# Shared-expert pieces of the last two images of a scan, mixture-of-experts and attention kernel, placed at other steps of the order

## The reference

```
x = x + scan(layernorm(x))          # 16 states per channel, h = exp(dt*a)*h + dt*b*x over 512 tokens
x = x + moe(layernorm(x))           # 64 experts, top 6, capacity 64 tokens per expert
x = x + attention(layernorm(x))     # 16 query heads, 4 key heads, causal
x = x + moe(layernorm(x))           # the same weights as the first time
...
def moe(hidden):
    y = routed experts: silu(x @ w_gate[e]) * (x @ w_up[e]) @ w_down[e], weighted and summed
    shared = silu(hidden @ sw_gate) * (hidden @ sw_up) @ sw_down      # inner width 704
    return y + shared
```

## Time and profile before

| | before |
|---|---|
| median of three runs | 3010.05 us |
| profiled execution | 3011.85 us, span 3010.0 us |
| TensorE busy | 2721.4 us (90%) |
| VectorE busy | 1790.6 us (59%) |
| GpSimd busy | 1529.4 us (51%) |
| ScalarE busy | 1298.4 us (43%) |
| last of the scans starts | 1044.7 us |
| experts' first transposes (L1116) start | 1116.60 us |
| end of the first experts on TensorE | about 1512 us |
| DMA, mean over the span | 188 GB/s |

### The profile page before, as it was taken

The page is one execution under the profiler, slowest core; times in us unless marked ns, Lnnn a source line. Parts: engine busy times, 40 slices in busy tenths (PEclk is TensorE's granted clock), DMA queues, the critical chain, the costliest instruction groups (busy, mean ns, idle before and its releaser), DMA issues.

```text
span 3010.0 us, 37439 instructions
## 1 busy us (share of the span) xinstructions
PE 2721.4 (90%) x13484; PEld 1435.5 (48%) x13484; DVE 1790.6 (59%) x3787; ACT 1298.4 (43%) x2689; POOL 1529.4 (51%) x944
## 2 busy tenths in 40 slices
PE   4658888998998879999969999999899999999998
PEld 2445554555555534433335555555544444444443
DVE  5899999999999852222246666665524444222222
ACT  4557585775857411111127767666712220111111
POOL 6999999999999901222135555554400001121211
PEclk7669999998999889999989999999999999999999
DMA  5454645545455379999930000001135324899997
GB/s 191 149 169 139 202 168 169 187 147 197 163 183 165 131 273 367 396 393 393 387 112 1 29 29 29 29 29 56 49 100 194 118 75 163 307 377 341 361 338 217
DMA packets 168234, 566.13 MB, mean 188 GB/s; under 512 B 22832, under 2 KB 24752, under 8 KB 167536
## 3 DMA queue, kind: packets, MB, share of 16 engines
q1 hardware_dynamic: 149904, 521.65, 46.9%
q0 software_dynamic: 17088, 40.90, 5.9%
q10 hardware_dynamic: 1056, 1.18, 0.1%
HBM read 487.89 MB, written 75.79 MB: 187 GB/s over the span
## 4 chain that ended last, share of the span: by engine, by line
PE 54%; ACT 3%; DVE 2%; POOL 2%; DMA 1%; issue 1%; POOLq 0%; SPq 0%; DVEq 0%; ACTq 0%
PE bank L1133 10%; PE bank L1159 5%; PE bank L1071 5%; PE bank L1036 5%; PE bank L1057 5%; PE bank L1184 5%; PE bank L1241 4%; PE bank L1218 3%; PE bank L1206 2%; PE bank L1230 2%; POOL arena L1940 2%; PE bank L1116 1%; PE bank L1172 1%; ACT arena L1763 1%; PE bank L1043 1%
## 5 line engine op out<-in xcount | busy, mean ns | idle before, releaser
L1844 POOL TENSOR_TENSOR arena<-arena 128x1024 f32<-128x1024 f32 x256 | 607.0, 2372 | 6.1 <-PE bank L986 3.0
L1692 ACT ACTIVATE bank<-arena 128x512 f32<-128x512 f32 x512 | 346.7, 689 | 317.9 <-DVE arena L1330 198.5
L986 PE MATMUL bank<-arena 128*128 128x128 f32 x2048 | 303.9, 301 | 147.3 <-POOL arena L1850 147.2
L1940 POOL TENSOR_TENSOR arena<-arena 128x2048 f32<-128x2048 f32 (+3 forms) x128 | 296.9, 2323 | 274.7 <-DVE arena L1560 274.6
L986 PEld LDWEIGHTS bank<-arena 128*128 128x128 f32 x2048 | 258.2, 155 | 233.5 <-POOL arena L1850 188.2
L1763 ACT ACTIVATE arena<-arena 128x256 f32<-128x256 f32 (+3 forms) x512 | 287.2, 566 | 148.3 <-DVE arena L1551 125.8
L1850 POOL TENSOR_TENSOR arena<-arena 128x512 f32<-128x512 f32 x256 | 333.6, 1304 | 17.5 <-DVE arena L1330 17.5
L1133 PE MATMUL bank<-arena 128*64 128x352 f32 x2048 | 327.2, 474 | 0.0
L1330 DVE TENSOR_TENSOR_SCAN arena<-bank,arena 128x512 f32<-128x512 f32 x256 | 310.7, 1214 | 25.9 <-POOL arena L1844 18.9
L1330 DVE TENSOR_TENSOR_SCAN bank<-bank,arena 128x512 f32<-128x512 f32 x256 | 308.4, 1205 | 0.0
L1057 PE MATMUL bank<-arena 128*128 128x512 f32 x640 | 288.3, 593 | 7.6 <-ACT arena L1719 7.6
(11 more groups left out here) (145 smaller groups left out, 4156.5 us busy)
## 6 DMA issues: line engine op xcount, KB each, us to landing
arena<-scratch_bc SPq DMA_DIRECT2D x128, 1024.0 KB, 5.4
arena<-in_w_out SPq DMA_DIRECT2D x128, 768.0 KB, 16.3
arena<-in_w_gate SPq DMA_DIRECT2D x128, 704.0 KB
arena<-in_w_up SPq DMA_DIRECT2D x128, 704.0 KB
scratch_x<-arena SPq DMA_DIRECT2D x16, 1024.0 KB, 4.5
scratch_xn<-arena SPq DMA_DIRECT2D x15, 1024.0 KB, 4.1
arena<-scratch_x SPq DMA_DIRECT2D x44, 256.0 KB, 6.1
arena<-scratch_x SPq DMA_DIRECT2D x8, 1024.0 KB, 7.5
```

What stands on the lines that cost most here:

```text
L986: i = nc.tensor.matmul(y[:, t * P:(t + 1) * P], w[:, n, t * P:(t + 1) * P], p.ident, is_transpose=True, start=False, stop=g == GROUPS - 1 ...
L1692: nc.scalar.activation(bank[p.da_bank(k, n)][:, :], block_of(p.dt, b, c), ACT.Exp, scale=p.alog[:, c, state:state + 1]).then_inc(*p.decaye ...
L1844: nc.gpsimd.tensor_tensor(out=p.hb[k % HB], in0=over(block_of(p.dtx, b, c), 1, NG), in1=p.bc[k // 2 % NBC][:, 0], op=ALU.mult).then_inc(*p ...
L1940: nc.gpsimd.tensor_tensor(out=own, in0=own, in1=over(p.rden[:, k % 2, :], 2, width), op=ALU.mult).then_inc(*p.divided.up(k))
```

## The change

The steps at which shared pieces stand become a table by image, `SHARED_AT`. Images 0 to 4 keep theirs. For image 5 the fourth down piece stands at step 46 instead of 51. For image 6 (the seventh) all gate and up pieces stand at steps 12 to 26 of the last batch, one at a time, and its down pieces at 29, 30, 33 and 34; the last two fall behind the last scan step, into the chain. In the chain, twelve pieces are made instead of eight: `sd` 2 and 3 of image 6, then `sg` and `su` of j = 0 to 4 of image 7. Five units are left for the experts' stage: j = 5, and t = 0 to 3 of image 7. The places at which products are read in the chain move with them. In the changed file every line behind the table is five to six lines further down.

```diff
+SHARED_AT = [(GATES, UPS, DOWNS)] * (BATCH - 3)
+SHARED_AT += [(GATES, UPS, (40, 41, 43, 46)), ((12, 15, 17, 20, 23, 26), (13, 16, 18, 21, 24, 26), (29, 30, 33, 34))]
...
-MADE_BESIDE = {"stats": 2, "logit": 1, "pick0": 1, "pick4": 1, "merge": 1, "lists": 1}
-TAKEN_BESIDE = {"rstd": ("silu",), "apply": ("hid",), "route_exp": ("silu",), "masks": ("hid",), "pick4": ("so",),
-                "merge": ("so",), "lists": ("so",)}
+MADE_BESIDE = {"stats": 2, "logit": 2, "pick0": 2, "pick4": 1, "merge": 2, "lists": 3}
+TAKEN_BESIDE = {"logit": ("so",), "route_max": ("so",), "route1": ("silu",), "pick1": ("silu", "hid"),
+                "merge": ("silu", "hid"), "lists": ("silu", "hid")}
...
+    gates, ups, downs = SHARED_AT[q]
     for j in range(SC):
-        yield GATES[j], ("sg", 0, q, j)
...
+        yield gates[j], ("sg", 0, q, j)
...
     products = [i for i in left if i[0] in ("sg", "su", "sd")]
+    products += [(kind, 0, BATCH - 1, j) for j in range(SC) for kind in ("sg", "su")]
+    products = products[:sum(MADE_BESIDE.values())]
```

More of the change, by code:

```diff
@@ L299, in quad_track @@
             yield PICK_AT[n], ("pick", 0, q // 2, n)
+    gates, ups, downs = SHARED_AT[q]
     for j in range(SC):
-        yield GATES[j], ("sg", 0, q, j)
-        yield UPS[j], ("su", 0, q, j)
-        yield GATES[j] + SILU_LAG, ("silu", 0, q, j)
-        yield UPS[j] + HID_LAG, ("hid", 0, q, j)
+        yield gates[j], ("sg", 0, q, j)
+        yield ups[j], ("su", 0, q, j)
+        yield gates[j] + SILU_LAG, ("silu", 0, q, j)
+        yield ups[j] + HID_LAG, ("hid", 0, q, j)
     for t in range(QT):
-        yield DOWNS[t], ("fetch", 0, q, t)
-        yield DOWNS[t], ("sd", 0, q, t)
-        yield DOWNS[t] + SO_LAG, ("so", 0, q, t)
+        yield downs[t], ("fetch", 0, q, t)
+        yield downs[t], ("sd", 0, q, t)
+        yield downs[t] + SO_LAG, ("so", 0, q, t)
 def first_steps():
```

## The result

The changed kernel is slower: 3031.05 us (median of 6, 3022.69 to 3036.72) against 3010.73 us for the kernel before (6 runs, 3007.67 to 3011.93), a ratio of 1.0056 with a 95% interval of 1.0043 to 1.0069. The forecast was 3025, with 3007 to 3036 as its range. The forecast lies between its two medians, and the difference is +20.3 us the first time and +10.7 the second.

What follows compares the result with a forecast made beforehand. DMA was taken to end last in the experts' stage, with TensorE closely matched. Transposes +16.9 us late, -3.4 at the stream's start, +1.5 at its end gave +15.0: 3026.9 for the execution, 3025 for the median, range 3007 to 3036.

Steps and rivals of the forecast that it cites:

- term 7: Experts' stage: -3.4 us from filling the stream's first gap, +1.5 us for a slow `up` at the end.
- Term 1: Last scan batch: GpSimd held 9.3 us in the middle, two down pieces before the last `x1`; `x1` +6.2 us.
- 2 turns: Start of the turns: two down pieces (10.9 us) behind the last sum instead of 6.9 us of pieces; +3.2 us.
- Term 3: Fold, behind `gate`: 6.9 us of pieces instead of a 3.44 us half-width pair and 2.41 us idle; +0.9 us.
- Term 4: Picks: `hid` 1 waits for `su` 1, whose bank `hid` 0 must free, with VectorE idle; +4.0 us.
- Term 5: `lists`: the `so` behind the merge that it waited for is gone; -0.65 us.
- Term 6: Barrier: three pieces, partly at low clock, and `hid` 4 end behind GpSimd's drain; +3.2 us.
- A: Rival, experts' stage: TensorE, not DMA, bounds it, so all 34.4 us come off; -17.5, 2993 us; chance 0.15.
- B: Rival, scan and chain: they take the pieces in, GpSimd held less, `hid` 1 finds its piece made; +4.0, 3014 us; chance 0.15.
- C: Rival, experts' stage: TensorE waits for weights, drops to 1.2 GHz and becomes the bound; 25 us more, 3050; chance 0.06.

Runs made afterwards that it cites:

- e2: Changed kernel with the two `hid` apart: `hid` 0 behind the first pick, `hid` 1 behind the fourth; 3019.58 us, ratio 1.0022.
- e5: Changed kernel with ten chain pieces instead of twelve, one down piece moved behind the gate, first `silu` and `hid` behind the fourth pick; 3029.88 us, ratio 1.0058.
- e6: Changed kernel without the three pieces between `lists` and the barrier, which go to the experts' stage; 3023.51 us, ratio 1.0035.
- c1: The changed kernel itself, word for word, timed again as a control; 3023.39 us, ratio 1.0036.
- e1: Changed kernel with only the two left-over down pieces in the chain and all ten units in the experts' stage; 3021.77 us, ratio 1.003.
- e4: Changed kernel loading only the first third of each expert's down weights from the seventh expert on, first mixture layer; 2971.46 us, ratio 0.9865.
- e3: Kernel before, loading only the first third of each expert's down weights from the seventh expert on, first mixture layer; 2992.46 us, ratio 0.993.
- e7: Kernel before with image 6's first four gate/up pairs at steps 17 to 26, image 5's last down at 46, experts' first unit one pair later; 3004.45 us.
- e8: Changed kernel's gate and up pieces, but down pieces and chain as in the kernel before; 3016.9 us, ratio 1.0014.
- e9: As e7, with the fourth up piece of image 6 at step 28 instead of 26; 3004.63 us, ratio 0.9972.

## Why the prediction was right, by its own steps

The sign, the size and the mechanism of the delay stood. That the time itself came so close is in part luck: the two medians of the changed kernel lie 7.7 us apart, and term 7 is right by two errors that cancel. Differences are of the two profiled executions.

| term | predicted | measured |
|---|---|---|
| brought along from earlier batches | 0 | +2.65 |
| 1 middle and two down pieces | +6.2 | +6.3 |
| 2 turns | +3.2 | +3.1 |
| 3 fold (13.50 against 13.16) | +0.9 | +0.3 |
| 4 picks (17.83 against 13.32) | +4.0 | +4.5 |
| 5 `lists` | -0.65 | -0.04 |
| 6 barrier (15.74 against 12.84) | +3.2 | +2.9 |
| transposes | +16.9 | +19.7 |
| 7 stage | -1.9 | -2.6 |
| behind the stage | 0 | +0.2 |
| span | +15.0 | +17.3 |

Without what was brought along, the transposes are late by 17.0 us and the span is 14.6 longer, against 16.9 and 15.0.

*Term 1.* Feed 246, held by 9.3 us in the working, was held by 11.7 - 2.65 = 9.05. The two down pieces behind step 251 then made up the end as worked out. One thing was not foreseen: in e2, e5 and e6, which have the same code there, `x1` came 1.7 us later still (81.0 us behind sum 234, against 79.3 in the changed kernel, c1, e1 and e4). In e2 the first of the two, behind a sum that waited 2.44 us for GpSimd, ran its 10 matmuls in 5.84 us, against 4.46, at a granted clock of 0.76 against 1.00. The same wait of 2.44 us stands there in the kernels that kept the full clock, so the wait alone does not decide it.

*Term 3* is half a microsecond off because the turns, with no `so` to wait for between them, took 0.4 us less up to the gate. Behind the gate it was +0.8, as worked out.

*Term 4* is the step that e2 proves: moving the place where VectorE asks takes 4.07 of its 4.5 us away. It was sized 0.5 short: 3.44 us for the piece became 3.86 us idle, which is 0.4 of it.

*Term 5* was mis-sized. The `so` is gone, but the merge's two matmuls, behind 5.70 us of idle TensorE, took 1.09 us instead of 0.62; that is 0.5 of the 0.6 us. The clock was looked for at the barrier and not here.

*Term 6.* TensorE ended behind GpSimd's drain, as expected. The low-clock piece took 5.25 us in place of 3.60, 1.7 more, against 2.3 in the working.

*Term 7.* The stage was paced by transfers, as the working said. Its two parts were both mis-sized, and the sum hides it. The first gap gave 5.3 us in place of 3.4, since the working took the half-width unit and not the clock of the first pair (6.45 us before, 4.95 now). From the second pair to the stage's end it took 2.7 us more than before (0.95 in c1), where +1.5 stood for one slow `up` at the end (the last one was 1.7 us slower: 6.65 against 4.95). The Trainium skill (DMA: Bandwidth & Descriptors, "Measured (HBM→SBUF, 128 partitions, SWDGE, issued from GpSimd)") has 425 GB/s for a 16 MB transfer on one core alone. A stretch of 5 us at the start comes near it, 423 GB/s from 1156 to 1161 us; over the long stretches the stream stood at 393 or 394 GB/s in the kernel before, the changed one, e1 and e6, whatever TensorE did, and that decides here.

*Rivals.* A is excluded by e1 and shown possible, with another stream, by e3 and e4. B needed transposes before 1122; they came at 1136.3, GpSimd was held 9.05 us and VectorE stood idle 3.86 us between the two `hid`. C's mechanism occurs (an `up` at 6.65 and one at 7.65 us above), and the granted clock of the stage's long first stretch fell from 1.00 to 0.95, but the stage stayed at DMA's pace, under 395 us. The Trainium skill (TensorE: Matmul & The Clock Gate, "HAM oscillation — how this bites in real kernels") describes such slices; here they cost nothing, since the weights are what is waited for.

Not settled: what moves the remainder behind the stage between 1493.4 and 1499.1 us, and why the changed kernel's two sets of 6 runs lie 7.7 us apart (3031.05 and 3023.39). The two profiles differ by 3.7 us: +2.7 at the transposes, -1.8 in the stage, -4.6 behind it.

## What to carry to other kernels

Before taking work off an engine, ask of the stage it stands in which resource ends last: 34 us of TensorE work were worth 2.6 us beside a full stream of weights, and those by an earlier start of the stream, and 34.9 beside a lighter one. Work moved into a latency chain costs what the chain's own engine waits for it, so place the point at which the product is read (e2) with as much care as the point at which it is made. Filler beside a chain has two prices, one where it stands in the way (turns +3.1 us) and one where it is missing (gate 7.06 us in place of 3.75); what won (e7) left the chain alone, kept pieces out of the last steps, and left steps without a piece between them, since a piece and a sum (4.3 us) take longer than the pacing engine's step (3.54). These were changed together, and the stages of e7's profile, not an experiment for each, say what each gave.

## What the runs showed of the hardware

Idle time of TensorE can cost more than itself. Behind turns with 1.90 and 1.26 us idle ahead of them (e5), or 7.25 us (e8), the gate took 7.06 us, and 3.75 in the changed kernel, where two down pieces and the turns stand in one row: near a factor of two, at a granted clock of 0.50 against 1.00, the two levels of 1.2 and 2.4 GHz. The last three sums (24 records) took 4.48 to 5.09 us behind waits for GpSimd (e7, e8, e9), against 2.84 with a piece ahead of them. But not every wait does it: behind the same wait of 2.44 us in the same order, a down piece's first ten matmuls took 4.46 us in the changed kernel, c1, e1 and e4, and 5.69 to 5.84 us in e2, e5 and e6.

The stream of weights held 393 or 394 GB/s at a DMA share of 1.03 while TensorE's busy share in the same 190 us went from 98% (before) over 96% (e1) to 90% (changed): in this stage TensorE's load did not disturb it. The share does not measure the rate: with the lighter loads of e4 it was 1.02 at 373 GB/s.
